# Summing the low halves of g in pairs on VectorE before TensorE sums them over the pixels

## The reference

```python
out = relu(bn(w_conv1 @ x))                   # 256 channels
d = relu(bn(w_dr @ out + b_dr))               # 128 channels, 3136 pixels
xc = d - mean(d, over the pixels)
cov = xc @ xc.T / 3136                        # 128 x 128 for each sample
r = einsum('cjh,bch->bcj', w_row, bn(cov)).reshape(B, 512) + b_row
att = sigmoid(w_fc @ r + b_fc)                # 256 numbers for each sample
return x * att
```

## Time and profile before

| | us |
|---|---|
| median of 3 runs | 1909.06 |
| lowest and highest | 1908.38, 1911.06 |
| profiled execution, its own time | 1908.1 |
| its span | 1906.3 |

### The profile page before, as it was taken

The page is one execution under the profiler, slowest core; times in us unless marked ns, Lnnn a source line. Parts: engine busy times, 40 slices in busy tenths (PEclk is TensorE's granted clock), DMA queues, the critical chain, the costliest instruction groups (busy, mean ns, idle before and its releaser), DMA issues.

```text
span 1906.3 us, 39985 instructions
## 1 busy us (share of the span) xinstructions
PE 1674.2 (88%) x13394; PEld 1316.7 (69%) x13394; DVE 1531.0 (80%) x2803; ACT 1498.7 (79%) x2276; POOL 462.0 (24%) x137
## 2 busy tenths in 40 slices
PE   8999999999991000489999999999999999999998
PEld 8999999999981000356667666676666766766664
DVE  6888888888877755577888888888888888888883
ACT  7777777777768997678887888878788787887876
POOL 6888888888860000000000000000000000000000
PEclk9999999999995555699999999999999999999999
DMA  9998999999969999401645645546455464554634
GB/s 333 373 371 312 373 349 331 375 332 345 377 250 430 430 430 430 190 2 69 215 170 175 220 161 211 179 163 230 155 212 184 154 238 156 201 192 154 232 113 203
DMA packets 139775, 477.37 MB, mean 250 GB/s; under 512 B 10576, under 2 KB 33232, under 8 KB 124752
## 3 DMA queue, kind: packets, MB, share of 16 engines
q1 hardware_dynamic: 139728, 476.75, 67.7%
HBM read 284.04 MB, written 192.68 MB: 250 GB/s over the span
## 4 chain that ended last, share of the span: by engine, by line
PE 56%; ACT 2%; DVE 1%; issue 1%; ACTq 0%; DVEq 0%
PE y_ps L890 18%; PE z_ps L916 17%; PE d_ps L866 14%; PE cov_ps L847 5%; ACT h L962 1%; PE ch_ps L901 1%; ACT hh L967 0%; PE ch_ps L879 0%; DVE g L1110 0%; PE ch_ps L878 0%; PE cov_ps L850 0%; ACT p_res L990 0%; DVE hl L1101 0%; ACT gg L954 0%; PE cov_ps L824 0%
## 5 line engine op out<-in xcount | busy, mean ns | idle before, releaser
L280 POOL TENSOR_TENSOR xl<-xs,xh 128x1568 fp32r<-128x1568 f32 x128 | 459.3, 3589 | 97.2 <-ACT xh L239 97.2
L1101 DVE TENSOR_TENSOR hl<-h,hh 128x1024 f16<-128x1024 f32 (+2 forms) x224 | 244.1, 1090 | 101.7 <-ACT hh L967 101.4
L890 PE MATMUL y_ps<-qr,udh 128*128 128x512 f16 (+2 forms) x896 | 314.5, 354 | 4.0 <-ACT p_res L990 3.6
L890 PE MATMUL y_ps<-qr,udl 128*128 128x512 f16 (+2 forms) x896 | 314.0, 354 | 0.0
L916 PE MATMUL z_ps<-qr,wl 128*128 128x512 f16 (+2 forms) x896 | 313.6, 353 | 0.0
L916 PE MATMUL z_ps<-qr,wh 128*128 128x512 f16 (+2 forms) x896 | 313.4, 353 | 0.0
L990 ACT ACTIVATE p_res<-y_ps,att_cy 128x512 f32<-128x512 f32 (+2 forms) x448 | 298.2, 713 | 11.0 <-PE y_ps L890 6.1
L239 ACT ACTIVATE xh<-xs 128x1568 fp32r<-128x1568 f32 x128 | 194.1, 1517 | 139.9 <-PE pp L297 139.8
L962 ACT ACTIVATE h<-z_ps,sb_h 128x512 f32<-128x512 f32 (+2 forms) x448 | 264.3, 626 | 27.5 <-PE z_ps L916 23.7
L866 PE MATMUL d_ps<-vh,hh 128*128 128x128 f16 (+1 forms) x1600 | 281.9, 219 | 2.3 <-DVE hl L1101 2.1
L866 PE MATMUL d_ps<-vh,hl 128*128 128x128 f16 (+1 forms) x1600 | 281.1, 219 | 0.0
(11 more groups left out here) (170 smaller groups left out, 2821.3 us busy)
## 6 DMA issues: line engine op xcount, KB each, us to landing
xs<-in_x_dram SPq DMA_DIRECT2D x128, 784.0 KB, 6.8
out_dram<-p_res SPq DMA_DIRECT2D x31, 3136.0 KB, 10.2
pt<-p_scratch SPq DMA_DIRECT2D x55, 1568.0 KB, 12.8
p_res<-p_scratch SPq DMA_DIRECT2D x112, 512.0 KB, 4.2
p_scratch<-po_low SPq DMA_DIRECT2D x56, 784.0 KB, 7.7
p_scratch<-late SPq DMA_DIRECT2D x56, 784.0 KB, 7.8
p_res<-p_scratch SPq DMA_DIRECT2D x56, 384.0 KB, 3.2
p_res<-p_scratch SPq DMA_DIRECT2D x28, 320.0 KB, 3.2
```

Of the source, the lines that this page charges most:

```text
L280: nc.gpsimd.tensor_tensor(xl[:, k % 2], xs[:, k], xh[:, k % 2].bitcast(F32), ALU.subtract).then_inc(split_done, 1)
L890: last = nc.tensor.matmul(y_ps[:, m, 0:widths[c]], part[:, k, m * P:(m + 1) * P], qr[:, slot, k, columns(c)], start=k == 0 and part is udh ...
L1101: nc.vector.tensor_tensor(hl[:, par, :, 0:w], h32[:, par, :, 0:w], hh[:, par, :, 0:w], ALU.subtract).then_inc(h_split, 1)
```

## The change

VectorE gets one more instruction in each chunk. Behind L1036 it waits for L1036 to finish (`g_split`), adds float16 low halves of `gg` in pairs of tiles into a new float16 buffer `low_sum`, and raises a new semaphore, `low_summed`. In a chunk of 4 tiles it adds tiles 0 and 2, and 1 and 3 (one instruction over 128 x 256 elements). In a chunk of 3 tiles it adds tiles 0 and 2, and in the last chunk tiles 0 and 1 (128 x 128 elements each).

TensorE waits on `low_summed` instead of `g_split` ahead of the chunk's covariance. It issues all the 257-column matmuls first and then the one-column matmuls: two of pair sums in a chunk of 4 tiles; one pair sum and tile 1 alone in a chunk of 3; one pair sum and the tile of 64 pixels alone in the last chunk. One-column matmuls for a sample go from 25 to 14.

```diff
+        low_summed = sem("low_summed")
+            low_sum = cb("low_sum", [P, 2, 2, P], F16)
+            def pairs(c):
+
+                full = widths[c] // P
+                return full // 2 if full <= 2 else full - 2
...
-                        pe.wait_ge(g_split, g - 1)
+                        pe.wait_ge(low_summed, g - 1)
...
                         for t in range(tiles[c]):
                             q = min(P, widths[c] - t * P)
-                            end = c == CH - 1 and t == tiles[c] - 1
                             nc.tensor.matmul(cov_ps[:, 0:2 * P + 1], gg[0:q, par, t, 0:P],
                                              gg[0:q, par, t, 0:2 * P + 1], start=c == 0 and t == 0,
                                              stop=False)
-                            last = nc.tensor.matmul(cov_ps[:, 2 * P:2 * P + 1], gg[0:q, par, t, P:2 * P],
-                                                    gg[0:q, par, t, 2 * P:2 * P + 1], start=False, stop=end)
+                        sums = [(P, low_sum[:, par, t]) for t in range(pairs(c))]
+                        if widths[c] // P == 3:
+                            sums.append((P, gg[:, par, 1, P:2 * P]))
+                        if widths[c] % P:
+                            q = widths[c] % P
+                            sums.append((q, gg[0:q, par, tiles[c] - 1, P:2 * P]))
+                        for n, (q, low) in enumerate(sums):
+                            last = nc.tensor.matmul(cov_ps[:, 2 * P:2 * P + 1], low,
+                                                    gg[0:q, par, 0, 2 * P:2 * P + 1], start=False,
+                                                    stop=c == CH - 1 and n == len(sums) - 1)
                         last.then_inc(cov_done, 1)
...
                         nc.vector.tensor_tensor(gg[0:dq, par, 0:dt, P:2 * P], g32[0:dq, 0:dt],
                                                 gg[0:dq, par, 0:dt, 0:P], ALU.subtract).then_inc(g_split, 1)
+                        dve.wait_ge(g_split, g - 1)
+                        n, other = pairs((s - 2) % CH), 2 if dw // P > 2 else 1
+                        nc.vector.tensor_tensor(low_sum[:, par, 0:n], gg[:, par, 0:n, P:2 * P],
+                                                gg[:, par, other:other + n, P:2 * P],
+                                                ALU.add).then_inc(low_summed, 1)
```

## The result

The changed kernel takes 1928.94 us (median; 1927.79 to 1929.69) against 1909.06. The ratio is 1.0103 with a 95% interval of 1.009 to 1.0117: slower. The forecast was 1926.5, within 1917 to 1940.

What follows compares the result with a forecast made beforehand. TensorE's stream was taken to bound the kernel, with little slack at its handovers. 0.06 + 0.16 + 0.40 - 0.08 = +0.54 us a sample over 31 samples, plus 0.7, gave +17.5 us: 1926.5 us, range 1917 to 1940.

Steps and rivals of the forecast that it cites:

- The bound: Steady part: PE's stream sets the time if others deliver; DVE's idle 15% is an average, slack at each handover counts.
- One-column matmuls: TensorE, chunks c0 to c5: ten fewer a sample at 0.028 us each, saving 0.28 us.
- The last chunk: TensorE's covariance of c6: four changes of row count make it 0.72 us instead of 0.56, +0.16 a sample.
- The passages: Changes between 128 and 64 rows in c6: about 0.10 us each; rival, free behind long matmuls, 1921 us, chance 0.08.
- The add: VectorE, each chunk: 0.28 us for 256 elements, 0.22 for 128, at the fast rate.
- The slow rate: Rival for VectorE's add: 0.42 us for 256 elements, 0.28 for 128; +28 us, 1937 us, chance 0.15.
- The argument by bytes read: VectorE's add: slow operations read eight bytes an element, the add four, so reads take half the time.
- The wait: VectorE's wait on `g_split` ahead of each add: 0.04 us beyond the add's length.
- Step 5: PE's d of c0 to y: two adds delay L1110 of c2 by 0.64 us, less 0.24 slack: +0.40 a sample.
- Step 1: PE's z of step 0 to covariance of c6: add of 0.26 us less 0.20 slack, +0.06 a sample.
- The rest: PE's y of step 5 to the next step 0: c3 and c4 save 3 x 0.028, -0.08 a sample.
- The count: Whole run: +0.54 us a sample in some 31 of 32 samples, 16.7 us, plus 0.7 for start and tail.

Runs made afterwards that it cites:

- VectorE's half alone: Kernel before plus all seven waits and adds a sample on VectorE, sums read by nobody, TensorE's matmuls as before: 1923.88 us, ratio 1.0081.
- c6 sorted: Changed kernel with the last chunk's matmuls sorted by rows, two passages between row counts instead of four: 1919.89 us, ratio 1.0062.
- no wait: Changed kernel, but the add takes the float16 high halves and doesn't wait for L1036: 1919.94 us, ratio 1.0063 to the kernel before.
- both sums on GpSimd: Kernel before with pair sums in c2 to c5 on VectorE and in c0 and c1 on GpSimd: 1906.24 us, ratio 0.9985.
- c0 and c2 to c5: Kernel before with pair sums in c0 and c2 to c5, all added on VectorE: 1909.32 us, ratio 1.0003.

## Why the prediction was right, point by point

**The bound.** PE's stream set the time before, and DVE's 15% of idle time didn't protect it. Right: VectorE's half alone costs 0.8%, though the adds' 59 us (37.4 + 21.6) are well inside the 160 us that it idled.

**One-column matmuls.** 0.028 us each was forecast, 0.027 measured, as the mean over a chunk (0.501 us for 4 + 2, 0.388 for 3 + 2).

**The last chunk.** Forecast +0.16, measured +0.19. The passages cost the 0.10 us also behind a long matmul, as sorting them away showed. The Trainium skill's statement that a weight load doesn't depend on the row count ("TensorE: Matmul & The Clock Gate", "LDWEIGHTS (loading the stationary operand)") agrees with the trace as to the load itself (0.09 us with 64 rows, 0.10 with 128), but is silent on a change of row count between neighbours. The trace decides for 0.1 us.

**The add.** 0.28 and 0.22 forecast, 292 and 225 ns measured. The slow rate is refuted. The Trainium skill's doubled rate for tensor_tensor on 16-bit operands ("VectorE: DVE Perf Modes", "The perf-mode tier table") holds: from 128 to 256 elements the add takes 67 ns more, 0.52 ns an element against 1.05. The argument by bytes read doesn't hold, and that it gave the right number is luck. L1036 and L1101 read one float32 and one float16 tensor, six bytes an element and not eight; in proportion to bytes the add would come to 0.70 ns an element and 0.33 us. The wait was put at 0.04 and the add's net cost for whatever follows at 0.32; measured are 0.03 and 0.33.

**Step 5.** Forecast +0.40, measured +0.43. The place, the path (VectorE's L1110 of c2, ScalarE, `y_free`) and the price were right. Two adds delay L1110 of c2 by 0.65 us, and the slack was 0.21 and 0.24 in the two samples of a loop turn. Leaving out two adds removed the wait; VectorE's half alone produced it.

**Step 1.** Forecast +0.06, measured +0.11, and this is the term that was read wrong. The slack of 0.20 was taken from one sample, the second of a loop turn. There the change costs 0.07, as in the written-out samples 4 and 5. In the first sample of each turn it costs 0.15, and the trace of before would have said so. One sample on from the earlier trace rows the same two instructions stand closer:

```profile
1266.86 0.56 DVE L1036 TENSOR_TENSOR gg<-g,gg 128x384 f16<-128x384 f32 x1 [0.67 <-ACT gg L954]
```
```profile
1267.59 0.27 PE L847 MATMUL cov_ps<-gg 128*128 128x257 f16 x1
```

L1036 ends at 1267.42 and PE starts 0.17 us later instead of 0.25, since ScalarE's L954 starts 0.11 behind the end of L1110 there and 0.03 in the other sample. The mean over both kinds of sample would have given +0.10.

**The rest.** Forecast -0.08, measured -0.03. After a wait the first matmuls of y in step 5 stand 0.01 us further apart, and in every second sample the first z of the next step 0 comes 0.07 us later. The latter falls on the turn of the engines' loop. The trace's records of TensorE's queue show the loop's branch and the register operations behind it ending 0.165 us ahead of that z in the changed kernel. In all five kernels that have this delay (the changed one, c6 sorted, no wait, both sums on GpSimd, c0 and c2 to c5) it is the same 0.165 us, and in the others, before included, the queue is through 0.18 to 0.65 us ahead and z isn't late. So z waits there for TensorE's own queue. Why the queue gets to the branch late in those five I haven't found.

**The count.** I multiplied 0.54 by 31 samples. In fact 24 loop samples cost 0.70, samples 4, 5 and 30 cost 0.25, and 2 and 3 only 0.02: their bytes needn't be quantised, so VectorE's stretch is shorter. The sum of +18.4 comes close to the forecast because the price was too low and the count too high; that closeness is partly luck. With 0.70 for all 31 the same sum would have given about 1931.5 us. I read slack in one loop sample and took all for alike. Without the loop's extra the change would have cost an estimated 7.5 us (0.25 for each sample from 4 on, and 0.7 in the first two).

## What to carry to other kernels

An engine's average idle time doesn't pay for new work. Follow each hand-over to the bound engine and compare its slack in hundredths of a microsecond with what is added ahead of it; work placed where the engine waits anyway cost nothing here (c2 to c5), and the same work in its full stretch costs all of its time beyond the slack. Read the slack in written-out samples and in each sample of a loop turn; here it differed by 0.08 us in step 1 and by 0.35 in step 5. When matmuls are reordered, count the changes of row count between neighbours. The tail of a matmul's row can hide a wait of up to 0.2 us: measure starts, not idle time.

## What the runs showed of the hardware

- Going from 128 to 64 rows in the stationary operand, or back, delayed the next matmul: 0.21 us instead of 0.11 behind a matmul of 257 columns, 0.10 instead of 0.03 behind one of one column. Four passages took 0.2 us more than two.
- A wait of VectorE on its own last instruction made the next start 0.03 us behind that one's end, instead of 0.08 ahead of it.
- In the loop, a wait on an engine's own last result followed by other waits cost 0.10 us more on VectorE and 0.15 on ScalarE than in written-out code.
- Where TensorE's queue reached the loop's branch late, the first matmul behind it started 0.165 us after the branch's register operations, up to 0.10 us late.
- A float16 add of 128 x 256 took 0.29 us on VectorE. On GpSimd it took 0.62 us, and 0.66 beside a VectorE scalar_tensor_tensor with both tensors in SBUF, which went from 0.48 to 0.72 us.
